# Attention rounds: the one-segment third burst of outputs joins the second, and the denominators of the preceding unit move from round 1 to the start of round 2

## The reference

```python
qk = x @ W_qk                       # x after layernorm; 16 heads of 64
q, k = jnp.split(qk, 2, axis=-1)    # each to (b, 16, n, 64)
scores = jnp.einsum('bhid,bhjd->bhij', q * BETA, k)
scores = jnp.where(causal_mask, mask_value, scores)
attn = jax.nn.softmax(scores, axis=-1)
out = jnp.einsum('bhij,bhjd->bhid', attn, k)   # the keys are the values
out = out.transpose(0, 2, 1, 3).reshape(b, n, HEADS * DIM_HEAD)
return out @ W_out
```

## Time and profile before

| | |
|---|---|
| time, median of 3 runs | 731.11 us (730.75 to 732.27) |
| time of the profiled execution | 732.0 us |
| its span, first to last instruction | 730.1 us |
| mean granted clock of TensorE | 0.989 |
| PE busy | 707.1 us, 97% |
| DVE / ACT / POOL busy | 60% / 50% / 57% |
| pitch of a unit of attention (units 1 to 13) | 26.4 us |

### The profile page before, as it was taken

One profiled execution on the slowest core, in us unless ns is written; L12 is line 12 of the kernel. 1 busy time (PEld: TensorE's weight loads), 2 busy tenths in 40 slices (PEclk: granted clock), 3 DMA queues, 4 the chain that ended last, 5 costly groups with the idle time before them and its releaser, 6 DMA issues. The chain is left out here.

```text
span 730.1 us, 14977 instructions
## 1 busy us (share of the span) xinstructions
PE 707.1 (97%) x5675; PEld 499.7 (68%) x5675; DVE 434.8 (60%) x1214; ACT 366.3 (50%) x474; POOL 417.5 (57%) x310
## 2 busy tenths in 40 slices
PE   7899999999999999999999998999999999899998
PEld 6665665666566666566566655988888865678887
DVE  6776766765775775676676511455654657755433
ACT  4465554655555555555465542354664343555421
POOL 4486686677568659659657765144544422354543
PEclk9699999999999999999999999999999999999999
DMA  2000001001001001100100111723223000043332
GB/s 72 8 16 23 26 21 28 24 17 30 24 15 30 23 19 27 29 17 23 27 17 17 31 44 29 177 89 112 97 77 109 1 0 1 6 142 103 105 103 72
DMA packets 41276, 33.49 MB, mean 46 GB/s; under 512 B 14002, under 2 KB 32756, under 8 KB 41204
## 3 DMA queue, kind: packets, MB, share of 16 engines
q1 hardware_dynamic: 41204, 32.52, 15.4%
HBM read 23.32 MB, written 1.31 MB: 34 GB/s over the span
## 5 line engine op out<-in xcount | busy, mean ns | idle before, releaser
L427 POOL TENSOR_TENSOR all_x<-all_x,at_probs 128x1024 f32<-128x1024 f32 (+3 forms) x128 | 208.2, 1627 | 19.0 <-ACT at_probs L525 0.4
L525 ACT ACTIVATE at_probs<-at_ring 128x1024 f32<-128x1024 f32 x144 | 144.3, 1026 | 99.9 <-PE at_ring L762 98.7
L587 DVE CUSTOM_DVE_ANT_0 at_ring<-at_ring,at_after_query 128x128 f32<-128x128 f32 (+3 forms) x252 | 116.9, 516 | 69.1 <-PE at_ring L716 69.1
L783 PE MATMUL at_both<-at_probs,at_k_nat 128*64 128x512 f32 (+1 forms) x736 | 134.3, 493 | 0.2 <-issue 0.2
L1280 POOL TENSOR_TENSOR m_prod<-m_gate,m_wb 128x512 f32<-128x512 f32 x64 | 81.6, 1280 | 87.5 <-ACT m_gate L1142 79.8
L427 POOL TENSOR_TENSOR all_x<-at_probs 128x768 f32<-128x768 f32 (+1 forms) x32 | 67.3, 2102 | 105.1 <-ACT at_probs L525 102.4
L583 DVE TENSOR_REDUCE at_half_max<-at_ring 128x2 f32<-128x1024 f32 x64 | 78.3, 1225 | 42.6 <-PE at_ring L716 42.6
L783 PEld LDWEIGHTS at_both<-at_probs,at_k_nat 128*64 128x64 f32 x736 | 47.0, 136 | 65.3 <-issue 54.5
L1196 DVE TENSOR_TENSOR m_hid<-m_prod,m_u 128x512 f32<-128x512 f32 x64 | 43.7, 686 | 73.5 <-POOL m_prod L1280 70.0
L1058 PEld LDWEIGHTS m_acc<-rest_wd,m_hid 128*128 128x128 f32 (+1 forms) x576 | 74.4, 191 | 7.8 <-DVE m_hid L1196 2.2
L1142 ACT ACTIVATE m_gate<-m_g 128x512 f32<-128x512 f32 (+1 forms) x72 | 42.6, 597 | 70.1 <-PE m_g L1049 68.8
(11 more groups left out here) (254 smaller groups left out, 1189.6 us busy)
## 6 DMA issues: line engine op xcount, KB each, us to landing
m_wb<-m_wt_far SPq DMA_DIRECT2D x128, 128.0 KB, 2.9
at_inv<-at_inv_q SPq DMA_DIRECT2D x240, 32.0 KB, 1.9
all_x<-in_L_attn_a_x SPq DMA_DIRECT2D x8, 256.0 KB, 3.8
at_w_raw<-in_L_attn_a_W_qk SPq DMA_DIRECT2D x8, 128.0 KB, 2.5
out<-all_x SPq DMA_DIRECT2D x4, 256.0 KB, 2.4
a_room<-in_L_attn_a_W_out SPq DMA_DIRECT2D x1, 512.0 KB, 4.2
m_raw_wg<-in_L_ffn_experts_wg SPq DMA_DIRECT2D x1, 512.0 KB, 3.8
m_raw_wu<-in_L_ffn_experts_wu SPq DMA_DIRECT2D x1, 512.0 KB, 3.9
```

The costliest lines, as they stand in the source:

```text
L427: return pool.tensor_tensor(sums[:, :, a * P:b * P], left, right, ALU.add)
L525: act.activation(probs[:, :, slot * BANK:(slot + 1) * BANK], pair("S", unit, slot)[:, :, :], ACT.Exp, scale=BETA).then_inc(exp_done, 1)
L587: last = dve.tensor_tensor_reduce(out=sums_ps, in0=sums_ps, in1=after_query[:, BANK - w:BANK], scale=1.0, scalar=MASKED, op0=ALU.add, op1= ...
L783: last = pe.matmul(out_bank(g, int(r > 0))[rows(l), o:o + (b - a) * P], k_nat[g % 3][:, j, rows(l)], probs[:, l, at:at + (b - a) * P], sta ...
```

## The change

The third burst of outputs, which has the single segment (4, 0), is added to the second one. There are now four bursts; `BURST_IN` says in which round each is made (rounds 0, 1, 3 and 4). Round 2 starts with `denominators(unit - 1, 1)` in place of outputs, and ACT's `invert(unit - 1, 1)` moves to round 2 with it. What hung on `NBURST - 1` as the last round now hangs on `LAST_ROUND`. `BURST_OF` and the counts on `av_done` follow from `BURSTS`.

```diff
-BURSTS = [[(0, 0), (1, 0), (2, 0), (1, 1)], [(3, 0), (2, 1)], [(4, 0)], [(5, 0), (6, 0)], [(7, 0), (8, 0), (8, 1)]]
+BURSTS = [[(0, 0), (1, 0), (2, 0), (1, 1)], [(3, 0), (2, 1), (4, 0)], [(5, 0), (6, 0)], [(7, 0), (8, 0), (8, 1)]]
 NBURST = len(BURSTS)
+
+BURST_IN = {0: 0, 1: 1, 3: 2, 4: 3}
...
+LAST_ROUND = len(ROUNDS) - 1
...
-            if r == NBURST - 1 and unit + 2 < UNITS:
+            if r == LAST_ROUND and unit + 2 < UNITS:
...
@@ scalar engine
-                        if r == 1 and unit:
+                        if r == 2 and unit:
                             invert(unit - 1, 1)
...
@@ matrix engine
                         if unit:
-                            outputs(unit - 1, r)
-                        if r == (1 if unit < UNITS else 3) and unit:
+                            if r in BURST_IN:
+                                outputs(unit - 1, BURST_IN[r])
+                        if r == (2 if unit < UNITS else 3) and unit:
                             denominators(unit - 1, 1)
```

More of the change, by code:

```diff
@@ L655, in _ @@
                             keys_low(dve, unit + 1)
-                        if r == NBURST - 1:
+                        if r == LAST_ROUND:
                             if more:
```

## The result

The changed kernel takes 733.47 us (median of 7 runs, the shortest 732.44 us) against 731.11 us: a ratio of 1.0029, 95% interval 1.0019 to 1.0040. It is slower by more than the measurement of this kernel leaves open. Experiment 5, the same kernel again on another occasion, gave 1.0039 (1.0026 to 1.0052). One of the seven runs, at 1714 us, is a disturbed one and left out of the ratio.

The account below looks back on a forecast made before the run. The prediction took PE's own list to bound the kernel. Fourteen waits of 0.08 us (1.1 us) plus 0.3 us in unit 15 gave +1.4 us on 731.11 us: 732.5 us, range 731.0 to 734.0 us.

Parts of the forecast that it names:

- What bounds the kernel: Whole kernel: PE is covered for 97% of the span, other engines for 60% or less, so PE's own list decides.
- What a block costs: PE in unit 7: a 512-wide segment costs 0.86 us, each burst 0.15 us more for beginning and end, denominators 0.57 us.
- steps 1 and 2: PE, rounds 1 and 2: masks, S1, S2 and M3 start 0.29 us later; M4 starts 0.15 us earlier.
- bound (0.42 or 0.72 us): Denominators at round 2's start: 0.42 us if the 0.15 us were saved, 0.72 us if it came twice, against 0.57 us.
- Step 3: S3 takes S2's bank pair: PE reaches it at 222.21 us, before S2's exponential on ACT ends at 222.29 us.
- Step 4: S3's second product follows the release by 0.39 us: 0.08 us longer in each of units 1 to 14.
- Unit 15: End of attention: S1's exponential starts POOL's chain of sums 0.29 us later, so the last denominators come 0.29 us later.
- What was costed at nothing: Moved reciprocals on ACT, SP's DMAs, M4's and M5's waits and the denominators' other waits were taken to add no time.
- The sum: Whole kernel: 1.1 us plus 0.3 us gives +1.4 us, 732.5 us, 0.19% up.
- the attention term: Units 1 to 14 of attention: 14 x 0.08 = 1.1 us from S3's wait.
- The faster rival: S3 does not wait, so the gain of 0.15 us per unit comes through: -1.8 us, 729.3 us; chance 13%.
- the slower one: Weight loads ahead of M4 are held for S1's exponential, 0.18 us per unit: 2.8 us more, 733.9 us; chance 22%.

Follow-up runs that it names:

- Experiment 5: The changed kernel run again with no edit, against the kernel before: 734.00 us, ratio 1.0039.
- Experiments 1: The changed kernel with M4's first product issued twice in units 1 to 14: 732.70 us, ratio 1.0018 to the kernel before.
- experiment 2: The changed kernel with denominators and reciprocals back in round 1, so only the bursts are merged: 743.16 us, ratio 1.0170 to the kernel before.
- experiment 4: The changed kernel with slot 2's exponential over half its columns in units 1 to 14: 730.53 us, ratio 0.9990 to the kernel before.
- experiment 3: The kernel before with denominators and reciprocals moved behind the burst of (4, 0) in round 2, five bursts kept: 731.41 us, ratio 1.0008.
- experiments 3 and 8: 8: experiment 3's kernel with unit 14's first output burst ahead of unit 15's transposed maxima, scale_out ahead of the last maxima: 729.90 us, ratio 0.9973.
- experiments 1, 2, 3, 5 and 6: 6: the kernel before, run again with no edit: 731.34 us, ratio 1.0001.
- experiment 9: The changed kernel with eight small matmuls filling PE's idle stretch ahead of unit 15: 732.58 us, ratio 1.0018 to the kernel before.

## Why the prediction was right, and where its sizes were off

- *What bounds the kernel.* Right. One row was misread: the 40 slices give the clock as 9, 6, 9, so it is the second slice (before unit 1) that is low, not the first. No term hung on it.
- *What a block costs; steps 1 and 2.* Right. The masks came 0.29 us later and the denominators cost 0.57 us in the new place, so neither bound (0.42 or 0.72 us) was needed. M4's lead was 0.18 us for a forecast of 0.15: the masks, M2, S1, S2 and M3 took 3.08 us where they took 3.11 us, and I had them unchanged.
- *Step 3, who is late next.* Right: S3, for S2's exponential, in each of units 1 to 14. Experiments 1, 2 and 4 show it from three sides: more work there is free, an earlier M4 behind later scores costs 0.64 us for each unit, a shorter exponential gives 0.23 us back.
- *Step 4, the price.* The mechanism is right, the term of 0.08 us was too large: 0.06 us by the pitch (0.04 us in experiment 5). The exponential ended 221.61 + 0.65 = 222.26 us by the old clock of the unit, for 222.29 forecast. Fourteen of these are 0.9 us, not 1.1.
- *Unit 15.* Forecast +0.29 us, measured 28.43 - 28.18 = +0.25 us from unit 15's start to the last denominators.
- *What was costed at nothing.* Right for the reciprocals (0.60 us of idleness left behind them), the DMAs (all issued by 222.36 + 10.01 + 0.65 = 233.02 us in the old clock of the unit, for 237.2 us at the latest), M5 and the denominators' waits; experiment 3 shows the first two by themselves.
- *The sum.* 1.4 us forecast, 1.17 us in the profile, 2.36 us (1.4 to 2.9 by the interval) in the medians. The forecast number lay at the low edge of what was measured, and that it came so near is in part luck, two errors that offset: the attention term was too large, and a term was missing.
- *The missing term.* It lies outside the repeated units. Of it, 0.35 us (0.47 us in experiment 5) is seen in the profile: the clock falls before the second mixture, a DMA goes out later, and the landings add scatter of their own, so the split between the two is not shown. The rest, 0.8 us by the medians and 1.2 us in experiment 5, is in no profile, and its cause stays open. A fall of the clock at a dearer place could be it: experiment 4's rows have one ahead of unit 15 for 1.7 us (4.04 - 2.37) and one at 640 us for 1.3 us. The mean clocks set a condition: executions of the changed kernel with spans of 732.5 and 732.7 us have the same 0.988 as the profiled ones of 730.6 and 730.9 us, so such a fall would have to stand in place of the one before the second mixture, or go with a shorter slow stretch ahead of unit 1, as in experiment 4 (two falls, 0.988). Up to 1 us can also lie ahead of unit 1, where the kernel before moves by that much. Why the clock falls in all these profiles of the changed kernel and in neither of the kernel before stays open too.
- *The rivals.* The faster rival did not happen; neither did the slower one by its own mechanism, although the time landed nearer to its side.

The Trainium skill's rule that a change of tiling mode drains the engine ("TensorEngine Tiling (Array Packing)", Key Properties) agrees with experiment 4: with the hold away, one block less saves 26.39 - 26.22 = 0.17 us for each unit. By that rule alone the change should have gained; the wait for a bank decided against it.

## What to carry to other kernels

When a list on the busiest engine is already without gaps, a block of work between two uses of a ring buffer is also the time in which another engine empties it. Before such a block is moved for a small saving of its own, take the end of the other engine's work and the start of the buffer's next use, shift each by what the move does to it, and see which comes first: 0.36 us of room was cut to nothing by a move of 0.29 us one way and 0.18 us the other. Where moving is wanted anyway, move a block to a place where the emptying engine gets more time, as experiments 3 and 8 do, and look for the one unit whose end another engine decides.

## What the runs showed of the hardware

- A weight load held by a semaphore starts 0.05 us after the end of the releasing instruction, on ACT (221.61 to 221.66 us, 225.37 to 225.42 us in experiment 2) as on DVE (40.77 to 40.82 us), and the next product of 512 columns comes 0.34 us after the load, where products otherwise follow each other by 0.24 us.
- The same 16-matmul burst took 2.37 us at full clock and 4.04 us behind an idle stretch of 1.75 us when the granted clock fell to 1.2 GHz. Kernels with the same idle stretch differed: it fell in experiment 4's profile and in none of those of the two kernels and experiments 1, 2, 3, 5 and 6.
- What a fall costs depends on what comes after it. Before the second mixture, ahead of a wait for DVE, PE had its lag of 1.4 to 1.6 us back at once, and 0.0 to 0.65 us was left at the end, by way of a DMA; behind that wait, in experiment 4, 1.3 us stayed.
- The mean granted clock orders the spans in experiment 3 (all six under 729 us have 0.989 or more, all six over 730 us have 0.988 or less) and in experiment 9, but not in the kernel before, which has 728.5 us at 0.988 and 730.3 us at 0.991.
